# Cross attention of batch 0 in steps of three score units and three product units on TensorE

## The reference, cut to what matters

```python
q = einsum('nqhd,od->nqho', layernorm(x) by heads, Wq);  k, v likewise of ctx_1024
energy = einsum('nqhd,nkhd->nhqk', q, k)           # 256 x 4096 for each head
attn = softmax(energy / 16, axis=3)                # the mask is all ones here
out = einsum('nhqk,nkhd->nqhd', attn, v).reshape(N, Sq, E) @ Wo.T + bo
x = x + out
```

## Time and profile before

| | |
|---|---|
| time, median of 3 runs | 1594.99 us (1594.75 to 1597.28) |
| the profiled execution's own time | 1597.6 us |
| its span | 1596.0 us |
| TensorE, VectorE, ScalarE, GpSimd busy | 86%, 79%, 61%, 26% of the span |
| granted TensorE clock, mean | 0.91 of 2.4 GHz |

### The profile page before, as it was taken

How to read it: one execution, slowest core, us unless ns; L and a number is a source line. 1 busy time by engine, 2 the same in 40 slices (tenths; PEclk the granted TensorE clock), 3 DMA queues, 4 the chain that set the end, 5 groups by cost and what they waited for, 6 DMA issues and landing times. The chain is left out here.

```text
span 1596.0 us, 31642 instructions
## 1 busy us (share of the span) xinstructions
PE 1371.6 (86%) x11762; PEld 854.5 (54%) x11762; DVE 1256.8 (79%) x3906; ACT 977.5 (61%) x1581; POOL 419.1 (26%) x316
## 2 busy tenths in 40 slices
PE   8999899999999999999968798688878778667746
PEld 4555566666666656666644584376456336423313
DVE  1353179998889998989998899998986785788993
ACT  6778677777777766777743353276585567443430
POOL 4110022222222222312212221312342342333350
PEclk9999999999999999999978899789978989777777
DMA  7876332133203320330105122115455256223330
GB/s 168 215 203 210 55 55 28 28 55 55 38 18 54 55 41 16 54 54 2 41 8 170 53 80 80 53 41 155 126 158 153 86 140 164 75 60 102 85 85 7
DMA packets 96856, 132.68 MB, mean 83 GB/s; under 512 B 20192, under 2 KB 80872, under 8 KB 93744
## 3 DMA queue, kind: packets, MB, share of 16 engines
q1 hardware_dynamic: 96688, 130.50, 32.5%
HBM read 124.95 MB, written 5.51 MB: 82 GB/s over the span
## 5 line engine op out<-in xcount | busy, mean ns | idle before, releaser
L1361 ACT ACTIVATE attn_arena<-ps 128x1024 f32<-128x1024 f32 x512 | 496.6, 1022 | 181.7 <-PE ps L421 180.5
L1966 DVE MATCH_REPLACE8 attn_late<-attn_shared,attn_late 128x256 f32<-128x256 f32 x1024 | 411.2, 409 | 0.0
L1963 DVE MAX8 attn_shared<-attn_late 128x8 f32<-128x256 f32 x1024 | 380.9, 414 | 23.9 <-ACT attn_late L1385 23.9
L421 PE MATMUL ps<-attn_arena 32*128 32x256 f32 x4096 | 371.3, 403 | 6.6 <-ACT attn_arena L1361 4.2
L421 PEld LDWEIGHTS ps<-attn_arena 32*128 32x128 f32 x4096 | 252.3, 186 | 71.5 <-issue 39.3
L435 PE MATMUL ps<-attn_arena 128*32 128x256 f32 x4096 | 277.4, 387 | 2.2 <-issue 1.6
L1224 POOL TENSOR_SCALAR attn_late<-attn_late 128x512 f32<-128x512 f32 x64 | 95.7, 1495 | 605.6 <-DVE attn_late L1966 605.6
L435 PEld LDWEIGHTS ps<-attn_arena 128*32 128x32 f32 x4096 | 107.8, 109 | 135.4 <-issue 73.5
L696 PE MATMUL ps<-attn_arena 128*128 128x256 f32 x512 | 134.5, 410 | 23.2 <-ACT attn_arena L1464 23.2
L674 PE MATMUL ps<-attn_arena,attn_q 128*128 128x512 f32 x256 | 133.6, 654 | 16.9 <-DMA attn_arena<-ctxT 8.9
L1237 POOL TENSOR_TENSOR attn_late<-attn_late 128x1024 f32<-128x1024 f32 x48 | 113.1, 2359 | 132.5 <-DVE ps L1789 130.1
(11 more groups left out here) (243 smaller groups left out, 1652.0 us busy)
## 6 DMA issues: line engine op xcount, KB each, us to landing
attn_arena<-ctxT SPq DMA_DIRECT2D x124, 256.0 KB, 4.6
attn_arena<-ctx SPq DMA_DIRECT2D x32, 512.0 KB, 4.2
attn_late<-rows SPq DMA_DIRECT2D x256, 64.0 KB, 2.3
attn_arena<-ctxV SPq DMA_DIRECT2D x15, 1024.0 KB, 13.0
attn_late<-maskT SPq DMA_DIRECT2D x20, 512.0 KB, 6.8
attn_late<-wide SPq DMA_DIRECT2D x64, 128.0 KB, 2.8
attn_early<-wide SPq DMA_DIRECT2D x64, 128.0 KB, 3.4
attn_arena<-maskT SPq DMA_DIRECT2D x12, 512.0 KB, 11.7
```

The costliest lines, as they stand in the source:

```text
L421: mm = pe.matmul(ps[:, first + j - 2 * i, u * S:(u + 1) * S], kx[n % 2][rows, k0:k0 + P], qpad[rows, n % GROUPS, b * S:(b + 1) * S], start ...
L1361: act.activation(probs[m % 2][:, 2 * i:2 * i + 2], ps[:, first:first + 2, :], ACT.Exp, scale=1.0 / 16.0).then_inc(exp_done, 1)
L1963: dve.max(top[:, t, turn], s[:, i, t] if turn == 0 else work[:, i, t]).then_inc(picked, 1)
L1966: dve.match_replace(work[:, i, t], top[:, t, turn], s[:, i, t] if turn == 0 else work[:, i, t], LOW).then_inc(picked, 1)
```

## The change

TensorE takes batch 0 in 11 steps a group instead of 16 iterations. A step `k` has the score units `3k` to `3k + 2` of the group (the eleventh has two, 30 and 31), and then the products of the step before it, now unit by unit (`unit_products`: both key tiles of two heads, four matmuls) with a wait on `exp_done` for each. Steps stand at the iterations 0, 2, 3, 5, 6, 8, 9, 11, 12, 14 and 15 of a group; the small blocks keep their slots. `pv_done` counts units instead of iterations. ScalarE's exponential of unit `u` waits in batch 0 for the products of unit `u - 4`, the last user of its half of `probs`. Before, the two units of iteration `m` waited together for the products of `m - 2`. From iteration 64 on the order is as before.

```diff
+STEP_ITS = 4 * PAIRS_OF_KT
+STEPS = (2 * PAIRS_OF_KT + 2) // 3
...
+            def unit_products(unit):
+                m, i = unit // 2, unit % 2
+                n, kk = m // PAIRS_OF_KT, m % PAIRS_OF_KT
+                if i == 0:
+                    values_due(n, kk)
+                pe.wait_ge(exp_done, unit + 1)
+                for u in range(2):
+                    for j in (2 * i, 2 * i + 1):
+                        mm = pe.matmul(acc[32 * j:32 * j + 32], values[n % 2][:, 2 * kk + u, j * VP:j * VP + 32], probs[m % 2][:, j, u * S:(u + 1) * S],
+                                       start=(kk == 0 and u == 0), stop=(kk == PAIRS_OF_KT - 1 and u == 1), skip_group_check=True)
+                mm.then_inc(pv_done, 1)
+
+            def step_units(n, k):
+                return [2 * PAIRS_OF_KT * n + unit for unit in range(3 * k, min(3 * k + 3, 2 * PAIRS_OF_KT))]
+
+            def cross_step(m):
+                n, at = m // PAIRS_OF_KT, m % PAIRS_OF_KT
+                for k in range(STEPS):
+                    if (3 * k + 1) // 2 == at:
+                        for unit in step_units(n, k):
+                            unit_scores(unit)
+                            if unit == 1:
+                                first_queries(range(1, GROUPS))
+                        for unit in step_units(n, k - 1) if k else step_units(n - 1, STEPS - 1) if n else []:
+                            unit_products(unit)
...
-                mm.then_inc(pv_done, 1)
+                mm.then_inc(pv_done, 2)
...
-                    if m is not None:
+                    if m is not None and m < STEP_ITS:
+                        cross_step(m)
+                    elif m is not None:
                         cross_scores(m)
-                        if m == 0:
-                            first_queries(range(1, GROUPS))
-                        if m:
-                            cross_products(m - 1)
+                        cross_products(m - 1)
...
             def cross_exp(m):
-                if m >= 2:
-                    act.wait_ge(pv_done, m - 1)
                 for i in range(2):
+                    if m >= 2:
+                        act.wait_ge(pv_done, 2 * m + i - 3 if m < STEP_ITS else 2 * m - 2)
                     act.wait_ge(scores_made, 2 * m + i + 1)
```

More of the change, by code:

```diff
@@ L400, in begin, with unit_scores, values_due @@
                 pe.wait_ge(misc_taken, misc[name])
-            def cross_scores(m):
+            def unit_scores(unit):
+                m, i = unit // 2, unit % 2
                 b, n, kk = m // 64, m // PAIRS_OF_KT, m % PAIRS_OF_KT
-                if n == 0 and kk in (0, FIRST_KT // 2):
+                if i == 0 and n == 0 and kk in (0, FIRST_KT // 2):
                     pe.wait_ge(k_first[1 if kk else 0], 64)
-                elif kk == 0:
+                elif i == 0 and kk == 0:
                     pe.wait_ge(k_loaded[n % 2], 64 * ((n + 1) // 2))
-                if m == 0:
+                if unit == 0:
                     pe.wait_ge(first_copied, 3)
-                if m == 1:
+                if unit == 2:
                     pe.wait_ge(q_copied, GROUPS - 1)
[L412 to L426, removed]
+                if last_user(unit) >= 0:
+                    pe.wait_ge(exp_done, last_user(unit) + 1)
+                first = unit_bank(unit)
+                for u in range(2):
+                    k0 = (2 * kk + u) * P
+                    for j in (2 * i, 2 * i + 1):
+                        rows = slice(32 * j, 32 * j + 32)
+                        mm = pe.matmul(ps[:, first + j - 2 * i, u * S:(u + 1) * S], kx[n % 2][rows, k0:k0 + P], qpad[rows, n % GROUPS, b * S:(b + 1) * S],
+                                       start=True, stop=True)
+                mm.then_inc(scores_made, 1)
+            def values_due(n, kk):
                 if kk == 0:
@@ L431, in cross_products, with cross_scores @@
                     pe.wait_ge(values_ready, 2)
+            def unit_products(unit):
+                m, i = unit // 2, unit % 2
+                n, kk = m // PAIRS_OF_KT, m % PAIRS_OF_KT
+                if i == 0:
+                    values_due(n, kk)
+                pe.wait_ge(exp_done, unit + 1)
+                for u in range(2):
+                    for j in (2 * i, 2 * i + 1):
+                        mm = pe.matmul(acc[32 * j:32 * j + 32], values[n % 2][:, 2 * kk + u, j * VP:j * VP + 32], probs[m % 2][:, j, u * S:(u + 1) * S],
[13 more added lines that the diff above has]
+                            unit_products(unit)
+            def cross_scores(m):
+                unit_scores(2 * m)
+                unit_scores(2 * m + 1)
+            def cross_products(m):
+                n, kk = m // PAIRS_OF_KT, m % PAIRS_OF_KT
+                values_due(n, kk)
                 pe.wait_ge(exp_done, 2 * m + 2)
@@ L1054, in _ @@
             sp.wait_ge(misc_taken, misc["heads", B - 1] + 1)
-            sp.wait_ge(pv_done, CROSS_ITS)
+            sp.wait_ge(pv_done, 2 * CROSS_ITS)
             for w, name in ((win, "win"), (wx, "wx"), (wout, "wout"), (alog, "alog"), (cw, "cw"), (cb, "cb"), (bdt, "bdt"), (dcol, "dcol")):
@@ L1105, in place_values @@
                 if n >= 2:
-                    pool.wait_ge(pv_done, PAIRS_OF_KT * (n - 1))
+                    pool.wait_ge(pv_done, 2 * PAIRS_OF_KT * (n - 1))
                 pool.tensor_copy(values[n % 2][:, :, 0:HG * VP].rearrange("p k (j v) -> p k j v", v=VP)[:, :, :, 0:D], vstage).then_inc(values_ready, 1)
@@ L1364, in copy_acc @@
                 b, g = n // GROUPS, n % GROUPS
-                act.wait_ge(pv_done, PAIRS_OF_KT * (n + 1))
+                act.wait_ge(pv_done, 2 * PAIRS_OF_KT * (n + 1))
                 if b:
```

## The result

The changed kernel is slower: 1631.89 us median against 1596.13 us for the kernel before, run beside it (each with one run some 11 us above its others), ratio 1.0242 with a 95% interval from 1.0194 to 1.029. The forecast was 1631. The profiled execution took 1632.21 us, 34.6 more than the 1597.6 of before.

A forecast was written before the change was run, and what follows sets the result against it. TensorE, in fixed order, was taken to set batch 0's pace. Group 0's 9.2, three groups of 9.3 and -1.0 for small blocks gave +36.1 us on 1597.6, or 1633.7; less 2.6 above the median, 1631 us, range 1616 to 1642.

The forecast's parts named there:

- The third unit: Batch 0's score and product blocks on TensorE: four more instructions on the fullest tiles cost 0.86 us, as much as a pair.
- The round through ScalarE's wait: Batch 0's steps: an exponential waits for products behind the same step's scores, so a step takes 4.21 us, not the array's 3.78.
- The end of a group: From step 9's products to those of the next group's second step: three steps take 10.66 us for 8 units.
- Group 0: Batch 0's first group, its start waiting for the queries: group 1 begins at 58.1 and not 48.95, +9.2 us.
- The small blocks: Short TensorE blocks between iterations of groups 1 to 3: partly hidden in steps' idle time, 11.4 us instead of 12.4.
- The exposed wait: make_q0 waiting in the open for DVE's copy (`misc_taken`), three times in batch 0: +0.87 us each, 2.6 in all.
- The sum: Whole kernel: group 0, three later groups and the small blocks together lose 36.1 us.
- the array alone decides: Rival for batch 0: ScalarE's wait is covered, a step takes 3.78 us; +23 us, 1618; chance 0.09.
- the switches decide: Rival for batch 0: fewer changes of form make it faster, at most -13 us, 1582; chance 0.03.
- gaps take the clock: Rival for batch 0: idle 0.43 us a step halves TensorE's clock for a fifth of it; +19 more, 1650; chance 0.04.

The follow-up runs named there:

- fifth_half: The changed kernel with a fifth half of probs in batch 0, so unit u's exponential waits for products of unit u - 5; median 1617.05 us, ratio 1.0088.
- thinned kernels: fifth_half without the second key tile of one unit in 37 steps, output not the reference's; third unit thinned 1599.64 us, second unit thinned 1624.44 us.
- one_group: The changed kernel with steps of three in group 0 alone, groups 1 to 3 in pairs; median 1607.35 us, ratio 1.0048.
- q0_apart: The changed kernel with batch 2's two make_q0 one slot later each, a step between them; exponential 32 to 64 took 50.6 us, against 51.9.

## Why the prediction was right

*The third unit, 0.86 us a block.* Right, and shown: 1.93 and 1.85 a block in fifth_half, and the pair of thinned kernels, which tell the fullest tile from the number of matmuls.

*The round through ScalarE's wait, 4.21 us a step.* Right in kind, shown by fifth_half; 0.05 too long, 4.16 measured. From the start of the products (102.93) the exponential begins 1.10 later (104.03) and not 1.16. I had taken the lag of ScalarE behind scores for its lag behind products. In the profile before, the last wait is a semaphore instruction of its own, ahead of the activation; here the wait on products sits on the activation itself. That the 0.05 comes from this was not tried.

*The end of a group, 10.66 us for 8 units.* In group 3's approach (no small block between) the products of step 9 of group 2 start at 151.33 in the trace, and those of the second step of group 3 at 161.96: 10.63.

*Group 0, +9.2.* Measured +9.1, in one_group +8.9. Part of this agreement is luck: eight rounds were 0.05 shorter than forecast, and the first scores behind the wait for the queries came 0.27 us later than before (16.24 against 15.97).

*The small blocks.* Hidden in the steps' idle time, and exposed where two stand together; shown at one place by q0_apart. The exposed wait was mis-sized a little: `turn_x0` to `make_q0` is 1.53 us (60.95 to 62.48, and again 112.89 to 114.42) and not 1.45, and between two `make_q0` it is 2.01 (89.65 to 91.66) and not 1.93. So each costs 0.94 us more than a hidden one, not 0.87. The 0.87 in the rows above is counted from the modelled end of the block before, 0.07 behind the point at which the next block could begin, so that its agreement with my 0.87 is an accident. Groups 1 to 3 took 142.3 us (201.56 - 59.25) where my terms add up to 144.4. Of the 2.1, 24 rounds that are 0.05 to 0.06 shorter make 1.3; the rest was not taken apart.

*The sum.* +36.1 forecast; +33.9 at the end of batch 0, +34.6 between the profiled executions, +35.8 between the medians. Of the 2.2 us missing at the end of batch 0 the profile has 0.8 again behind it. The other 1.2 between profiles and medians lies inside the spread of a kernel's runs, so that 1631.89 lands within 1 us of 1631 is partly luck; the sum was right to about 2 us.

*The rivals.* That the array alone decides, +23 us, did not come true in the changed kernel, but did in the profile of fifth_half, with +23.3 at the end of batch 0. (That its profiled execution took 1618.4 us and the rival said 1618 proves little, since the runs spread by more.) That the switches decide fell: fewer switches save 1.8 us a group (5 x 0.37), while each of the ten full steps needs 3.78 of the array alone where 1.5 iterations took 3.29, 4.9 us a group. The Trainium skill's rule on the drain at a change of mode (TensorEngine Tiling (Array Packing), Key Properties) agrees with the trace: from the start of a block's last score instruction to the products it is 0.304 or 0.305 us in 44 of 45 blocks. But what prices the block between two changes is that the tiles work independently, which the same section states and the thinned kernels bear out. That gaps take the clock did not happen in batch 0 of the changed kernel (1.00 throughout).

## What to carry to other kernels

In this kernel, a block of matmuls on row or column tiles, between two changes of form, lasts as long as its fullest tile. So count instructions by tile before making blocks longer to save changes: 20 instructions cost as much as 24 while two tiles kept eight each, and 0.43 us less once no tile had more than six. By the same rule 32 over four full tiles would cost no more than these 24; that was not run. And when a block grows, follow each buffer ring through it: with three bank pairs and four halves of `probs`, the third unit put a wait on the second exponential that only products behind the same block could end.

A fifth half of the buffer takes that wait away, but no version here that computes the reference beats the pairs of the kernel before. A unit cut by key tile over all four heads would fill the tiles evenly; as each head's scores go to a bank of their own in this code, it would need four banks at a time of the six; it was not tried.

## What the runs showed of the hardware that I had not expected

A stop of TensorE of 1.6 us, with nothing waited for, in the middle of dense work was followed by 6.8 us at half the clock (one_group), and lengthened that stretch by about 5 us; the same kernel's next profile had no such stop. A stop of that length doesn't always do this: 1.80 us from 871.0 us on, between other matmuls of the same profile, left the clock at 1.00 (868 to 875 us). And the full clock came at 15.0, 16.1 and 23.7 us in executions with nearly the same start, worth 3 us at 23.7. Differences of a few microseconds between single profiles of this kernel can be such events, and the clock should be looked at before they are explained.
